# A new plan of the extra pieces in an attention kernel's first nine steps, with routing's exponential moved into a step

## The reference, cut to what matters

```python
xn = layernorm(x)                                # x: 4 batches x 1024 rows x 128 columns
q, k = rope(xn @ Wq.T), rope(xn @ Wk.T)          # 16 heads of 8 columns
attn = softmax(q @ k.T / sqrt(8)) @ (xn @ Wv.T)  # for each batch and head
gate = softmax(xn @ gate_w + gate_b)             # 8 experts, the best 2 of each row
moe  = sum over the best 2: gate * expert(xn)    # three layers with gelu between them
out  = x + attn + moe
```

## Time and profile before

| | |
|---|---|
| Median of 3 runs | 666.11 us (666.0 to 669.47) |
| The profiled execution's own time | 665.8 us |
| Its span, first to last instruction | 664.1 us |
| Busy: PE, ACT, DVE, POOL | 619.4, 559.2, 243.4, 222.0 us |
| Granted TensorE clock, mean | 0.99 of full |

### The profile page before, as it was taken

How to read it: one execution, slowest core, us unless ns; L and a number is a source line. 1 busy time by engine, 2 the same in 40 slices (tenths; PEclk the granted TensorE clock), 3 DMA queues, 4 the chain that set the end, 5 groups by cost and what they waited for, 6 DMA issues and landing times.

```text
span 664.1 us, 12748 instructions
## 1 busy us (share of the span) xinstructions
PE 619.4 (93%) x4234; PEld 271.1 (41%) x4234; DVE 243.4 (37%) x699; ACT 559.2 (84%) x626; POOL 222.0 (33%) x235
## 2 busy tenths in 40 slices
PE   8689999999999999888999999998999999999995
PEld 5223432322232222222888888883222222222221
DVE  5573346552232332202555555550203021220304
ACT  3689898899999999999555555558999999999995
POOL 2501013317767766540122211224242333324300
PEclk9799999999999999999999999998999999999999
DMA  7793014323433333396333433421122121112204
GB/s 218 198 388 112 18 47 144 112 80 127 138 125 124 123 119 119 127 283 164 64 76 71 79 71 71 87 52 41 51 72 72 40 72 55 55 48 79 63 9 131
DMA packets 84057, 68.56 MB, mean 103 GB/s; under 512 B 47280, under 2 KB 61136, under 8 KB 84016
## 3 DMA queue, kind: packets, MB, share of 16 engines
q1 hardware_dynamic: 77328, 53.78, 27.6%
q0 software_dynamic: 5968, 13.51, 6.6%
q10 hardware_dynamic: 720, 0.71, 0.4%
HBM read 33.51 MB, written 33.42 MB: 101 GB/s over the span
## 4 chain that ended last, share of the span: by engine, by line
PE 56%; ACT 21%; issue 13%; DVE 5%; DMA 2%; POOL 1%; ACTq 1%; SPq 0%; POOLq 0%; DVEq 0%
ACT probs L610 14%; PE ps L1192 13%; PE ps L1215 10%; ACT probs L576 7%; PE ps L1177 6%; PE ps L1225 5%; PE ps L1208 5%; PE ps L1298 5%; PE ps L1145 4%; PE ps L1282 3%; PE ps L1201 2%; PE ps L1110 1%; DVE xn_all L684 1%; DMA q_st<-parts 1%; DMA b_raw<-in_L_ffn_b_dram 1%
## 5 line engine op out<-in xcount | busy, mean ns | idle before, releaser
L576 ACT ACTIVATE probs<-ps 128x1024 f32<-128x1024 f32 x288 | 273.4, 1032 | 18.3 <-PE ps L1177 12.8
L610 ACT ACTIVATE probs<-ps 128x1536 f32<-128x1536 f32 (+1 forms) x154 | 202.1, 1447 | 0.9 <-PE ps L1282 0.8
L1192 PE MATMUL ps<-probs,v_st 128*32 128x512 f32 x1152 | 154.3, 608 | 12.2 <-ACT probs L576 8.5
L591 ACT ACTIVATE work<-ps,work 128x256 f32<-128x256 f32 x156 | 70.7, 475 | 65.6 <-PE ps L1215 65.1
L1298 PE MATMUL ps<-probs,v_st 128*32 128x512 f32 x896 | 120.5, 611 | 0.6 <-ACT probs L610 0.6
L513 POOL DMA_INDIRECT work<-slots_y_d,slot_i x64 | 60.4, 944 | 117.0 <-PE ps L1298 64.3
L1282 PE MATMUL ps<-q_st,k_st 32*128 32x512 f32 x448 | 77.7, 497 | 13.9 <-ACT probs L610 13.1
L1177 PEld LDWEIGHTS ps<-q_st,k_st 32*128 32x128 f32 x576 | 28.0, 183 | 128.7 <-ACT probs L576 100.1
L1177 PE MATMUL ps<-q_st,k_st 32*128 32x512 f32 x576 | 73.6, 500 | 6.8 <-DMA q_st<-parts 3.9
L1282 PEld LDWEIGHTS ps<-q_st,k_st 32*128 32x128 f32 x448 | 29.1, 182 | 119.9 <-ACT probs L610 108.8
L473 POOL DMA_INDIRECT slots_x_d<-xn_all,slot_i x64 | 62.1, 971 | 46.7 <-PE ps L1192 32.0
(11 more groups left out here) (147 smaller groups left out, 448.4 us busy)
## 6 DMA issues: line engine op xcount, KB each, us to landing
k_d<-parts SPq DMA_DIRECT2D x8, 1024.0 KB, 5.6
q_d<-parts SPq DMA_DIRECT2D x8, 1024.0 KB, 4.9
q_st<-q_d SPq DMA_DIRECT2D x30, 256.0 KB, 3.0
k_st<-k_d SPq DMA_DIRECT2D x30, 256.0 KB, 2.8
slots_x_d<-parts SPq DMA_DIRECT2D x5, 1024.0 KB, 11.7
work<-slots_x_d SPq DMA_DIRECT2D x80, 64.0 KB, 2.3
slots_y_d<-work POOLq DMA_DIRECT2D x39, 128.0 KB, 2.2
parts<-in_L_ffn_w_dram SPq DMA_DIRECT2D x16, 128.0 KB
```

Of the source, the lines that this page charges most:

```text
L576: nc.scalar.activation(probs[:, j % PROB_RING, 2 * pair:2 * pair + 2, :], score_slot(j, pair).rearrange("p (h n) -> p h n", h=2), ACT.Exp, ...
L591: ins = nc.scalar.activation(dst[:, par, k, :], src[k][:, 0:ST], ACT.Gelu, bias=b12_st[:, par, n, k:k + 1])
L610: nc.scalar.activation(group_probs(phase, g)[:, 0:size, :], group_slot(g)[:, 0:size * HALF].rearrange("p (h n) -> p h n", n=HALF), ACT.Exp ...
L1192: ins = nc.tensor.matmul(o_ps[32 * h:32 * h + 32, :], v_st[:, mt, h, :], probs[:, j % PROB_RING, h, :], start=(mt == 0), stop=(mt == MT - 1))
```

## The change

1. The `values` pieces of batches 1 to 3 have two row tiles each, so four pieces for a batch in place of three.
2. The plan is worked out: the pieces of batches 1 to 3 fill every block from (0, 10) on that has no turn. `norm` 0 and 1 stand at (0, 7) and (0, 8), where the first `rows` pieces stood; those are at (0, 10) and (0, 11).
3. VectorE normalises batch 1's rows alone after the first piece, batch 2's after block (0, 11), batch 3's after block (1, 3).
4. Routing's stretch 0 stands at (2, 4), in place of (1, 11); `count` at (2, 15), right behind stretch 8 at (2, 14). Before, stretch 8 stood at (2, 10) and `count` at (2, 12).
5. ScalarE takes routing's exponential in step 2, between blocks 4 and 5, in place of between steps 1 and 2.
6. The five clearing transfers are issued in step 1, blocks 2 to 6.
7. The first keys are loaded in two transfers, 128 columns and then 384.
8. TensorE gets idle-time products: one of 64 columns of zeros after each of batch 0's eight row turns, and four of 512 columns (`WARM_AGAIN`) ahead of the first scores.

```diff
+def value_tiles(b, n):
+    return range(3 * n, min(3 * n + 3, BT)) if b == 0 else range(2 * n, 2 * n + 2)
 def plan_jobs():
-    jobs = {(0, 0): ("values", 0, 2), (0, 7): ("rows", 1, 0), (0, 8): ("rows", 1, 1), (0, 10): ("values", 1, 0),
...
+    turns = {BLOCKS * t + MT + 1 for t in range(SPLIT)} | {BLOCKS * t + 1 for t in range(1, SPLIT)}
+    fixed = {0: ("values", 0, 2), 7: ("norm", 0), 8: ("norm", 1), BLOCKS * 2 + 15: ("count",), BLOCKS * 7 + 12: ("bound",)}
+    first = rows(1) + vals(1) + [("norm", 2)] + rows(2) + [("norm", 3)] + vals(2) + rows(3) + vals(3)
+    first += pieces(4) + pieces(5) + [("norm", 4)] + pieces(6) + [("norm", 5)] + pieces(7)
+    places = free(10, 60)
+    fixed.update(zip(places, first))
...
-ROUTE = {(1, 11): 0, (2, 0): 1, (2, 2): 2, (2, 3): 3, (2, 4): 4, (2, 5): 5, (2, 6): 6, (2, 7): 7, (2, 10): 8, (2, 13): 9, (2, 14): 10,
+ROUTE_EXP = (2, 5)
+for _n, _block in enumerate([36] + [n for n in range(38, 60) if n % MT and n != 47][:18]):
+    ROUTE[divmod(_block, BLOCKS)] = _n
...
-            first_load(0, S["ka_loaded"])
+            first_load(0, S["k00_loaded"], 0, P)
+            first_load(0, S["ka_loaded"], P, HALF)
...
+                    if t == 1 and 2 <= j < 2 + SLOT_ROOM // 8:
+                        r = j - 2
+                        sp.wait_ge(S["scores_done"], t * UNITS + 2 * j)
+                        sp.dma_start(slots_x_d[r * 8 * ST:(r + 1) * 8 * ST, :].rearrange("(p a j) c -> p a (j c)", p=P, a=4),
+                                     parts[:, :, 3, :].bitcast(F32)).then_inc(S["x_zeroed"], 16)
...
             with act.Fori(0, 2) as t:
                 attention_exps(t)
+            attention_exps(ROUTE_EXP[0], 0, 2 * ROUTE_EXP[1])
             act.wait_ge(S["max_made"], 1)
             nc.scalar.activation(rt[:, 1], rt[:, 0], ACT.Exp).then_inc(S["exp_made"], 1)
-            with act.Fori(2, SPLIT) as t:
+            attention_exps(ROUTE_EXP[0], 2 * ROUTE_EXP[1])
+            with act.Fori(3, SPLIT) as t:
                 attention_exps(t)
...
+                    if (t, j) in ((0, 11), (1, 3)):
+                        prepare_rows(2 + t)
...
+                nc.tensor.matmul(aux_ps[:, 0:C // 2], zeros[:, 0:P], zeros[:, 0:C // 2], start=True, stop=True)
...
+            for _ in range(WARM_AGAIN):
+                nc.tensor.matmul(bank(0), zeros[:, 0:P], xnT[:, 0, 0:HALF], start=True, stop=True)
             pe.wait_ge(S["proj_read"], 4)
```

More of the change, by code:

```diff
@@ L55 @@
 WARM = 10
+WARM_AGAIN = 4
 def heads_of(g):
@@ L89, in plan_jobs, with pieces @@
-    early = [(1, j) for j in (13, 14, 15)] + [(2, j) for j in (0, 2, 3, 4, 5, 6, 7, 8, 10, 11, 13, 14, 15)] + [(3, j) for j in (0, 2, 3, 4)]
-    later = [(3, j) for j in (6, 8, 11, 13, 14)] + [(t, j) for t in (4, 5, 6) for j in (0, 2, 3, 5, 6, 8, 10, 11, 13, 14)]\
-        + [(7, j) for j in (0, 2, 3, 5, 6)]
-    for b in range(1, B):
-        row, norms = [], [("norm", 4 * b + k) for k in range(4)]
-        for k in range(4):
-            row += [(kind, 4 * b + k, part) for kind in ("plain", "swap") for part in range(2)]
-            if k and b > 1:
-                row.append(norms.pop(0))
-        for place, job in zip(early if b == 1 else later[20 * b - 40:], row + norms):
-            assert place not in jobs
-            jobs[place] = job
+    def pieces(g):
+        return [(kind, g, part) for kind in ("plain", "swap") for part in range(2)]
@@ new lines, in rows, with vals, free @@
+    def rows(b):
+        return [("rows", b, half) for half in range(2)]
+    def vals(b):
+        return [("values", b, n) for n in range(BT // 2)]
+    def free(lo, hi):
+        return [n for n in range(lo, hi) if n not in turns and n not in fixed]
+    turns = {BLOCKS * t + MT + 1 for t in range(SPLIT)} | {BLOCKS * t + 1 for t in range(1, SPLIT)}
+    fixed = {0: ("values", 0, 2), 7: ("norm", 0), 8: ("norm", 1), BLOCKS * 2 + 15: ("count",), BLOCKS * 7 + 12: ("bound",)}
+    first = rows(1) + vals(1) + [("norm", 2)] + rows(2) + [("norm", 3)] + vals(2) + rows(3) + vals(3)
@@ new lines, in plan_jobs @@
+    first += pieces(4) + pieces(5) + [("norm", 4)] + pieces(6) + [("norm", 5)] + pieces(7)
+    places = free(10, 60)
+    fixed.update(zip(places, first))
+    last = max(n for n, job in fixed.items() if job[0] == "swap")
+    assert last <= 3 * BLOCKS + 5, last
+    todo = [("norm", 6), ("norm", 7)]
+    for g in range(8, 16):
+        todo += pieces(g)
+        if g % 4:
+            todo.append(("norm", g - 1))
+        if g % 4 == 3:
+            todo.append(("norm", g))
+    places = free(last + 3, BLOCKS * 7 + 8)
@@ L101, in plan_jobs @@
+    step = (len(places) - 1) / (len(todo) - 1)
+    fixed.update((places[int(step * i)], job) for i, job in enumerate(todo))
+    jobs = {divmod(n, BLOCKS): job for n, job in fixed.items()}
     for t in range(SPLIT):
@@ L109, with plan_scatter @@
 AUX = {job: n for n, job in enumerate([JOBS[p] for p in sorted(JOBS)] + [("turn", SPLIT - 1, 1)])}
-ROUTE = {(1, 11): 0, (2, 0): 1, (2, 2): 2, (2, 3): 3, (2, 4): 4, (2, 5): 5, (2, 6): 6, (2, 7): 7, (2, 10): 8, (2, 13): 9, (2, 14): 10,
-         (2, 15): 11, (3, 2): 12, (3, 3): 13, (3, 4): 14, (3, 5): 15, (3, 6): 16, (3, 7): 17, (3, 10): 18}
+ROUTE_EXP = (2, 5)
+ROUTE = {}
+for _n, _block in enumerate([36] + [n for n in range(38, 60) if n % MT and n != 47][:18]):
+    ROUTE[divmod(_block, BLOCKS)] = _n
+def plan_scatter():
+    routed = max(t * BLOCKS + j for t, j in ROUTE)
+    swaps = [t * BLOCKS + j for (t, j), job in JOBS.items() if job[0] == "swap" and job[2]]
+    starts, n = {}, routed
+    while len(starts) < TILES:
+        if n not in swaps and n - 1 not in swaps:
+            starts[n] = len(starts)
+            n += 1 + (len(starts) % 8 == 0)
+        n += 1
+    return starts
 EXPERT_LOADS = (2, 3, 4, 5, 6, 7, 9, 10)
```

56 lines of the change are left out of this document (27 added, 29 removed).

## The result

| | before | after |
|---|---|---|
| Median | 666.06 us (665.59 to 669.47, 4 runs) | 673.78 us (671.7 to 675.25, 4 runs) |
| Ratio to before | 1 | 1.0095, 95% interval 1.007 to 1.0121 |
| Profiled execution, its span | 665.8, 664.1 us | 673.1, 671.4 us |

The account below looks back on a forecast made before the run. Blocks without pieces were taken as bound by ScalarE, step 2's full ones by TensorE. Gains of -5.8 us and losses of +5.9 on the profiled 665.8 gave 665.9 us, range 661.8 to 668.9.

Parts of the forecast that it names:

- A: First scores: new products may keep TensorE's clock up and delay nothing; -1.0 us, bounds 0 and -2.0.
- B: Block (0, 10): normalising batch by batch removes ScalarE's stall; -2.1 us, bounds -2.2 and -1.8.
- C: Batches 1 to 3: `values` pieces of two tiles instead of three shorten blocks; -0.6 us.
- D: Steps 2 and 3: VectorE's late reads and the `copy_o` wait go; -2.1 us, bounds -2.1 and -1.5.
- E: Block (2, 4): ScalarE waits for routing's stretch 0 on VectorE, held up by GpSimd; +3.0 us.
- F: Behind the wait for stretch 0 in step 2: TensorE's clock falls; +1.3 us, bounds 0 and +1.7.
- G: Block (2, 15): `count` waits for the masks of stretch 8; +1.3 us, bounds +0.3 and +1.4.
- H: Block (3, 8): `copy_o` late behind stretches 13 to 15 and a last swap part; +0.3 us.
- new order of the other pieces: Pieces other than the split `values`: reordering costs nothing, each still in a block of its own; 0 us.
- the rest: 64-column products, split key transfer (bounds -0.5 and +0.5) and moved clearing transfers: taken at nothing.
- rival 2: First nine steps: the clock never falls; A becomes -2.0 and F nothing, 663.6 us; chance 0.16.
- Rival 4: Behind (2, 5): low clock lasts 6.7 us as at the start; 669.0 us, or 670.3; chance 0.08.

Follow-up runs that it names:

- e8: Kernel before with only the normalising done batch by batch: 674.63 us, ratio 0.9971 to the kernel before.
- e1: Changed kernel with routing's stretch 0 at block (2, 2) in place of (2, 4): 666.68 us, ratio 0.9856 to the kernel before.
- e2: Changed kernel with `count` at block (3, 0) in place of (2, 15): 670.96 us, ratio 0.9933 to the kernel before.
- e3: Changed kernel with no routing stretch at blocks (3, 5) to (3, 7): 675.09 us, ratio 0.9964 to the kernel before.
- e17: e3 with an indirect scatter in every second block, so the last comes ten blocks earlier: 688.83 us, ratio 1.0162 to the kernel before.
- e13: e10 with routing stretches 9 to 18 later, stretch 9 behind the output sums' copy at (3, 0): 666.75 us, ratio 0.9983 to the kernel before.
- e4: Changed kernel with the edits of e1, e2 and e3 together: 667.68 us, ratio 0.9891 to the kernel before.
- e10: Changed kernel replanned: stretch 0 at (2, 1), its exponential after block 2, `count` at (2, 14), other stretches moved: 667.63 us, ratio 1.0009 to the kernel before.
- e11: Changed kernel with the scatters at the old spacing: 672.2 us, ratio 1.008 to the kernel before.
- e7: Changed kernel without the four 512-column products ahead of the first scores: 673.72 us, ratio 0.9972 to the kernel before.
- e12: Kernel before, unchanged, run again for a profile: 667.98 us.
- e16: e11 run a second time: 673.76 us, ratio 1.0084 to the kernel before.
- e6: Changed kernel, unchanged, run again beside the kernel before: 673.33 us, ratio 0.9949 to it.
- e18: e13 with an indirect scatter in every second block: 684.86 us, ratio 1.0125 to the kernel before.

## Why the prediction was wrong

Its steps against what the traces and the runs gave, in us at the start of step 8:

| term | forecast | measured | from |
|---|---|---|---|
| A, clock at the start | -1.0 (0 to -2.0) | -2.1 | block (0, 2): 30.31 to 28.24 |
| B and C | -2.7 | -3.1 | block (0, 2) to step 2: 63.07 to 59.94; e8 for B |
| D, VectorE's late reads | -2.1 | -1.9 | blocks (2, 8), (2, 9) and (3, 1): 8.14 to 6.28 |
| E and F | +4.3 | +4.7 to +4.9 | e1; blocks (2, 4), (2, 6), (2, 7) |
| G | +1.3 | +1.3 to +1.9 | e2; block (3, 0): 2.06 to 3.91 |
| H | **+0.3** | **+3.8 to +3.9** | e3, e17; blocks (3, 9), (3, 10) |
| new order of the other pieces | 0 | +1.4 to +2.3 | steps 4 to 7; with the lower figures above, 0.9 more in steps 2 and 3 |
| sum | +0.1 | +5.0 | 288.75 - 283.73 |

**The step that failed is H**, "between nothing and the 1.26 seen at (3, 0) I take +0.3, since there is one more free block". The stall was named and put in its right place; its size was wrong by a factor of more than twelve, 3.8 to 3.9 us in place of 0.3. I had the two things that make it: from L842 that a two-input operation takes 1.50 behind a last swap part, and from E that an idle of such length brings the clock down. I used both for E and F and neither for H. Six operations of about 0.42, four of them stretched by GpSimd's work, are 5.8 us; from the end of the high part at 141.6 the copy was due, done, at 145.9, 4.3 later. At 0.42 each, six and the copy would have been 3.3. "One more free block" was read as room, and gave none: the stretches planned for three blocks ran in one go beside GpSimd's work, and two blocks passed at 1.8 instead of 2.06, which brought the copy's time 0.5 nearer. What a free block does by itself was not tried; with only stretch 13 at (3, 6) and none at (3, 5) and (3, 7), in e13, the wait is at most 0.5. The bound was wrong too: 1.26 was a wait behind another amount of work, no bound for this one.

**The second miss is in "I cost their new order at nothing, because each still stands in a block of its own"**: steps 4 to 7 take 125.6 us in place of 124.3, and 125.6 to 126.2 in e4, e10 and e11. Part of it is C's own price, come due late. There are three `values` pieces more (102 pieces and turns in place of 99), and steps 0 to 2 have 42 in both kernels, so the three push others into later blocks that were free: step 3 has 13 in place of 11, steps 4 to 7 have 45 in place of 44. At 0.27 for a block, the forecast's own figure, that is 0.5 in step 3 and 0.3 in steps 4 to 7, which C's term had counted and which the -3.1 up to step 2 does not hold yet. For the rest, some 1.1 in steps 4 to 7, what differs is where the free blocks stand; I have no experiment on which of them costs, so its cause stays open.

**E, F, G** were right in mechanism, in place and nearly in size. L858 took 1.04 and not 1.50: it began 1.00 behind the start of `rotate` and not 0.56, and ended 0.27 behind `rotate`'s end, as forecast. The Trainium skill (SBUF — State Buffer, Who interferes with whom) says that a VectorE instruction with two SBUF inputs waits out a GpSimd instruction that reads SBUF and one with a single input, outside VectorE's two-port modes, doesn't; here the reduction L857 took 0.41 during `rotate`, L858, L882, L902 and L903 1.04 to 1.50, and L909, after GpSimd was done, 0.42. The trace agrees. This was the rule that H needed.

**A** came out at its far bound, in part by luck. The clock stayed up, through a wait of 1.29 for the first exponential; but in e3 and e13, the same there, it fell, so the doubt that the forecast's middle value stood for was right. And "they delay nothing" was wrong: the products held the scores up by 1.1 (e7), which only the scores' earlier start, put at nothing under "the rest", made good by as much. Of rival 2's two halves one came true; the other, that the clock would not fall in step 2, did not. Rival 4, a low stretch behind (2, 5) as long as the start's, came in e11 and e17 (6.83 us from 102 on, step 2 then 38.7 to 38.9 long) and not in the changed kernel's own profiles (3.41). Rows at either level, in the changed kernel's profile: 1.00 from 20.20 to 30.20, 0.50 at 104.60 and at 149.00, behind idles of TensorE of 3.01 and of 2.34; none behind the 1.38 at (2, 15). The Trainium skill (TensorE: Matmul & The Clock Gate, HAM oscillation) ties the fall to one idle stretch longer than any of these, and by it F and what the clock adds to H would be nothing; the two rows at 0.50 speak against it.

**The rest of the measured difference** lies behind step 8. The two profiles differ by 7.3 us and their eighth steps by 5.0; 2.3 more come between step 8 and the end, where the low stretch behind the experts is 10.24 us long in place of 3.41. It cannot be shown to be the change's doing: in e12, the kernel before, it is 10.24 as well, with this row:

```profile
454.50:464.50 10.00, 9.50 (x43) 2.04 (x42) 0.00 (x0) 6.91 (x6) 4.67 (x5) 0.50 0.14 39
```

and over the profiles of both kernels it is 3.41, 6.83 or 10.24. e12's span is 666.3, and 671.4 - 666.3 = 5.1 is the eighth step's difference again. The ratio's interval, 4.7 to 8.1 us, holds both.

**The sign.** Where the kernel before takes 666 to 668, the changed kernel of the first result, and e11 and e16 (the same with the scatters spaced as before), are slower by 0.8 to 1%; where it takes 676, the changed kernel is faster by 0.5% (e6). All of that turn is in the kernel before: its three stalls, each behind a burst of scatters. The change spaces the scatters out (a part that I did not cost at all), and it had no stall there (e6, and e1, e2, e4 and e7 of its kin), where the kernel before lost about 8 us by three. For bursts as the cause stand e3 and e17, which differ in the scatters alone, both where the kernel before takes 676 and more: one burst and 1.5 us lost, seven bursts and six stalls. Why only at some times, and how a burst of scatters makes signals from TensorE late, no run here settles; the changed kernel itself was not run beside e17 and e18.

**A version that beats both** was not found. e13 is level with the kernel before where that takes 667 (0.9983, 0.9962 to 1.0004), and e1 and e4 are 1.4 and 1.1% ahead of it where it takes 676. Its remaining loss, 3.9 us at the experts' start, would want earlier scatters without bursts; no run has both.

## What to carry to other kernels

When work of a lesser engine is planned by block, add up what stands ahead of each thing that the critical engine waits for, with each operation at its length under contention, and do not count a block with nothing in it as room before the sum is made. Where the same pattern occurs at four places, price it the same way at all four, the small ones too. And measure a baseline on more than one chip, and again later, before a change of one per cent is called anything: here it moved by 1.5% and the changed kernel by 0.1%. Last, when a piece is split, ask where the blocks that it takes will be missing.
